# Seven products for eight over pairs of batches, and y moved by transfers

## The reference

```python
W = weights[condition]                        # 16 matrices of 64x64, one per batch
y = jnp.einsum('bct,bcd->bdt', x, W)          # 64 x 64 x 1024
gate_logits = jnp.einsum('bsd,ed->bse', y, gate_w)            # 8 experts
weights, selected = jax.lax.top_k(gate_logits, 2)
weights = jax.nn.softmax(weights, axis=2)
result = jnp.einsum('bsd,od->bso', y, base_w) + base_b        # 1024 x 1024
low = jnp.einsum('bsd,erd->ebsr', y, lora_A)                  # 8 experts of rank 16
lora_out = jnp.einsum('ebsr,eor,bse->bso', low, lora_B, w_full)
return x + result + 2.0 * lora_out
```

## Time and profile before

| | |
|---|---|
| median of 3 runs | 493.68 us (493.53 to 493.83) |
| the profiled execution's own time | 493.63 us |
| its span in the profile | 491.5 us |
| PE, ACT, DVE, POOL busy | 99%, 78%, 75%, 26% of the span |

### The profile page before, as it was taken

How to read it: one execution, slowest core, us unless ns; L and a number is a source line. 1 busy time by engine, 2 the same in 40 slices (tenths; PEclk the granted TensorE clock), 3 DMA queues, 4 the chain that set the end, 5 groups by cost and what they waited for, 6 DMA issues and landing times.

```text
span 491.5 us, 8738 instructions
## 1 busy us (share of the span) xinstructions
PE 487.2 (99%) x2771; PEld 478.5 (97%) x2771; DVE 371.0 (75%) x801; ACT 382.3 (78%) x740; POOL 129.4 (26%) x111
## 2 busy tenths in 40 slices
PE   9999999999999999999999999999999999999997
PEld 8999999999999999999999999999999999999996
DVE  4987878778787778787787777787877787777654
ACT  4888878878778887778787788887788877887620
POOL 2033302333113333033332223332133320233121
PEclk9999999999999999999999999999999999999999
DMA  8812122231221221221222222312213212211112
GB/s 334 353 43 74 74 91 96 55 97 59 87 91 64 85 96 52 92 91 53 96 64 82 89 79 70 96 53 91 91 53 96 84 62 88 96 54 55 55 44 85
DMA packets 31986, 43.89 MB, mean 89 GB/s; under 512 B 18402, under 2 KB 22370, under 8 KB 31970
## 3 DMA queue, kind: packets, MB, share of 16 engines
q1 hardware_dynamic: 31826, 43.17, 25.7%
q10 hardware_dynamic: 144, 0.52, 0.3%
HBM read 25.00 MB, written 18.68 MB: 89 GB/s over the span
## 4 chain that ended last, share of the span: by engine, by line
PE 93%; ACT 3%; DMA 2%; DVE 1%; SPq 0%; issue 0%; ACTq 0%
PE acc L658 79%; PE acc L691 9%; PE mixed L678 6%; DMA w_raw<-in_proj_w 2%; ACT y_moved L370 1%; ACT w_raw L362 1%; DVE w_raw L474 0%; ACT x_parts L357 0%; ACT w_hi_rows L343 0%; SPq L225 0%; SPq L221 0%; DVE y_turned L481 0%; ACT y_hi L393 0%; DVE w_raw L560 0%; SPq L218 0%
## 5 line engine op out<-in xcount | busy, mean ns | idle before, releaser
L658 PE MATMUL acc<-w_hi_rows,y_hi 128*128 128x384 f32 (+3 forms) x768 | 256.5, 337 | 0.1
L658 PE MATMUL acc<-w_hi_rows,y_lo 128*128 128x384 f32 (+3 forms) x768 | 256.4, 337 | 0.0
L658 PE MATMUL acc<-w_lo_rows,y_hi 128*128 128x384 f32 (+3 forms) x768 | 256.0, 337 | 0.0
L370 ACT COPY y_moved<-w_raw 32x256 f32<-32x256 f32 x480 | 194.2, 405 | 37.8 <-DVE w_raw L474 32.0
L302 POOL TENSOR_TENSOR w_raw<-x_sb,bias 128x1024 f32<-128x1024 f32 x32 | 77.0, 2409 | 344.2 <-DVE low L529 258.5
L658 PEld LDWEIGHTS acc<-w_hi_rows,y_hi 128*128 128x128 f32 x768 | 143.9, 188 | 3.7 <-ACT w_hi_rows L343 0.4
L658 PEld LDWEIGHTS acc<-w_lo_rows,y_hi 128*128 128x128 f32 x768 | 143.9, 188 | 3.1
L658 PEld LDWEIGHTS acc<-w_hi_rows,y_lo 128*128 128x128 f32 x768 | 143.9, 188 | 0.6 <-DVE y_lo L459 0.3
L474 DVE TENSOR_TENSOR w_raw<-mixed,w_raw 64x1024 f32<-64x1024 f32 x60 | 73.0, 1217 | 30.0 <-ACT w_raw L362 29.6
L481 DVE STREAM_TRANSPOSE y_turned<-y_moved 128x512 f32<-128x512 f32 x60 | 42.3, 706 | 51.5 <-ACT y_moved L370 51.5
L362 ACT COPY w_raw<-mixed 64x1024 f32<-64x1024 f32 x60 | 60.8, 1014 | 20.9 <-PE mixed L678 20.2
(11 more groups left out here) (56 smaller groups left out, 238.5 us busy)
## 6 DMA issues: line engine op xcount, KB each, us to landing
x_sb<-in_x SPq DMA_DIRECT2D x32, 512.0 KB, 3.5
out<-w_raw SPq DMA_DIRECT2D x31, 512.0 KB, 2.6
w_raw<-in_proj_w SPq DMA_DIRECT2D x8, 580.0 KB, 9.6
scratch<-low_squares SPq DMA_DIRECT2D x29, 64.0 KB, 1.5
lowT_raw<-scratch SPq DMA_DIRECT2D x116, 16.0 KB, 1.8
cw<-in_cond_w ACTq DMA_DIRECT2D x1, 512.0 KB, 3.6
lb_raw<-in_lora_b SPq DMA_DIRECT2D x1, 512.0 KB, 16.4
bias<-in_base_b SPq DMA_DIRECT2D x1, 512.0 KB, 17.1
```

Source lines behind the costliest of these rows:

```text
L370: done = nc.scalar.copy(y_moved[q * SQ:(q + 1) * SQ, g, :, :], piece.rearrange("m (k q a) -> m q k a", q=QUARTERS, a=SQ)[:, q, :, :])
L658: return nc.tensor.matmul(acc[:, c % 2, b, 0:hi - lo], y_part[:, c % 2, k, :], w_part[:, k, lo:hi], start=(k == 0 and product == 0), stop= ...
```

## The change

The kernel now goes in 16 *steps* of two pairs each (pair 0 and pair 1 of the step). On 256 + 136 = 392 columns (`plain`) both pairs are projected as before. On the other 768 columns, the two pairs (rows), two halves of k, and two blocks of 384 columns make a 2 x 2 by 2 x 2 product of blocks. Step 0 does it with eight products (`multiply`, 4 x 3 = 12 matmuls of 384 columns each), all later steps with seven, which need four sums of blocks of y (`make_sums`, on POOL), four sums of blocks of w (once, on POOL), four snapshots of a bank that is still summed up (`snap`, on ACT) and three additions of snapshots to `res` (`add_snaps`, `add_third`, `add_fourth`, on POOL).

```diff
+            def step(j, u, ahead=True):                      # PE
+                plain_pair(j, u, 0)
+                mix(j, u, 0)
+                plain_pair(j, u, 1).then_inc(plain_done, 1)
+                mix(j, u, 1)
+                pe.wait_ge(res_ready, 2 * s)
+                multiply(C22, half(0, 0), factor(B11)).then_inc(prod_done, 1)
+                multiply(C11, half(0, 1), factor(B21)).then_inc(prod_done, 1)
+                mix(j, u, 2)
+                multiply(C22, summed(S2), factor(T2), first=False).then_inc(prod_done, 1)
+                multiply(C21, half(1, 1), factor(T4)).then_inc(prod_done, 1)
+                mix(j, u, 3)
+                multiply(C22, summed(S3), factor(T3), first=False).then_inc(prod_done, 1)
+                multiply(C12, summed(S4), factor(B22)).then_inc(prod_done, 1)
+                multiply(C22, summed(S1), factor(T1)).then_inc(prod_done, 1)
...
+            def plain_pair(j, u, i):                         # PE
+                if i == 0:
+                    pe.wait_ge(tails_added, s)
...
+            def mix(j, u, i):                                # PE
+                pe.wait_ge(x_split, m + 1)
+                pe.wait_ge(sel_ready, 2 * m + 2)
+                if u > 0 or i > 0:
+                    pe.wait_ge(sum_done, m)
```

`mix` now takes 128 rows at once with a w_sel of high and low parts, two matmuls for each batch, four batches in a step. The sum of a pair goes to one buffer `y_sum`, and the 16 pieces are moved by 16 transfers on SP's queue:

```diff
-            def move(j, c, b, pieces):                       # ACT
-                act.wait_ge(sum_done, 8 * j + 2 * (c - 2) + b + 1)
-                for i in pieces:
-                    done = nc.scalar.copy(y_moved[q * SQ:(q + 1) * SQ, g, :, :],
...
+            def move(j, u, i):                               # SP
+                sp.wait_ge(sum_done, 4 * s + 2 * i + 2)
+                if u > 0 or i > 0:
+                    sp.wait_ge(turned, 4 * s + 2 * i)
+                for g in range(QUARTERS):
+                    for q in range(QUARTERS):
+                        sp.dma_start(y_moved[q * SQ:(q + 1) * SQ, g, :, :].rearrange("m k a -> m (k a)"),
+                                     y_sum[g * SQ:(g + 1) * SQ, q * RUN:(q + 1) * RUN]).then_inc(moved[i], 16)
...
+            def step(j, u, ahead=True, load=True):           # SP
+                store(j, u - 1, i)                           # i = 0, 1
+                sp.wait_ge(bias_added, 2 * s + i + 1)
+                load_x(j, 2 * u + 4 + i)                     # i = 0, 1
+                move(j, u, 0)
+                turn_low(j, u)
+                move(j, u, 1)
...
+            def rest(j, u, i):                               # ACT
+                act.wait_ge(mix_done, 4 * s + i + 1)
+                if i < 2 and u > 0:
+                    act.wait_ge(moved[1], 16 * MOVES * s)
+                if i >= 2:
+                    act.wait_ge(moved[0], 16 * MOVES * (s + 1))
+                nc.scalar.copy(y_sum[here, :]..., mixed[there, :, :]).then_inc(rest_ready, 1)
...
+            def make_sums(j, u):                             # POOL
+                pool.wait_ge(turned, 4 * s)
+                pool.wait_ge(prod_done, 7 * s)
...
+            def step(j, u, ahead=True, split=True):          # POOL
+                make_sums(j, u)
+                select(j, u, 2)
+                s_low(j, u, S3)
+                s_low(j, u, S1)
+                add_bias(j, u, 0)
+                add_bias(j, u, 1)
+                select(j, u, 3)
+                add_snaps(j, u)
+                select(j, u, 4)
+                select(j, u, 5)
+                add_third(j, u)
+                add_fourth(j, u)
```

More of the change, by code:

```diff
@@ L16 @@
 SCALING = 32.0 / 16.0
+BW = 384
+SQ = 32
+QUARTERS = P // SQ
+B11, B21, B22, T1, T2, T3, T4 = range(7)
+S1, S2, S3, S4 = range(4)
 def adaln_ffn_kernel(
@@ L272, in _ @@
-            for i in range(4):
-                sp.wait_ge(stored[i], 16 * (PAIRS // 4 + (2 if i == LAST % 4 else 0)))
+            step(0, LAST - 1, load=False)
+            step(0, LAST, ahead=False, load=False)
+            store(0, LAST, 0)
+            for n, cols in enumerate((slice(BW, O), slice(0, BW))):
+                sp.wait_ge(res_ready, 2 * LAST + 2 + n)
+                sp.dma_start(out_pairs[2 * LAST + 1, :, cols], res[:, 1, cols]).then_inc(stored[1], 16)
+            for i in range(2):
+                sp.wait_ge(stored[i], 16 * (STEPS + i))
@@ L328, in _ @@
+            step(0, 1)
             with pool.Fori(0, LOOPS) as j:
-                for u in (5, 6, 7, 8):
+                for u in (2, 3):
                     step(j, u)
-            for n in range(PAIRS - 3, PAIRS):
-                step(0, n, ahead=(n + 2 < PAIRS))
-            add_bias(0, LAST)
+            step(0, LAST - 1, split=False)
+            step(0, LAST, ahead=False, split=False)
         @block.scalar
@@ new lines, in _, with step @@
+            rest(0, 0, 1)
+            x_high(0, 0, 3)
+            t_high(2, T1)
+            lowT_high(0, 0)
+            rest(0, 0, 2)
+            t_high(3, T2)
+            y_high(0, 0, 0, 0)
+            y_high(0, 0, 0, 1)
+            rest(0, 0, 3)
+            t_high(4, T4)
+            x_high(0, 0, 4)
+            x_high(0, 0, 5)
+            y_high(0, 0, 1, 0)
+            y_high(0, 0, 1, 1)
+            def step(j, u, ahead=True, split=True):
+                s_high(j, u)
+                if ahead:
+                    rest(j, u, 0)
+                    x_high(j, u, 2)
+                    rest(j, u, 1)
+                gate_exp(j, u)
+                if ahead:
+                    x_high(j, u, 3)
+                snap(j, u, 0, 1)
@@ L441, in _ @@
+                if not ahead:
+                    snap(j, u, 2, 5)
+                lowT_high(j, u)
+                if ahead:
+                    rest(j, u, 3)
+                if split:
+                    x_high(j, u, 5)
+                if ahead:
+                    snap(j, u, 2, 5)
+                snap(j, u, 3, 7 if ahead else 6)
+                if ahead:
+                    y_high(j, u, 1, 0)
+                    y_high(j, u, 1, 1)
+            step(0, 1)
             with act.Fori(0, LOOPS) as j:
-                for u in (4, 5, 6, 7):
+                for u in (2, 3):
@@ new lines, in first_step, with all_experts @@
+                mix(0, 0, 2)
+                multiply(C22, half(1, 1), factor(B22)).then_inc(prod_done, 1)
+                mix(0, 0, 3)
+                multiply(C22, half(1, 0), (b12_hi, b12_lo), first=False).then_inc(prod_done, 1)
+                pe.wait_ge(lb_ready, 1)
+                pe.wait_ge(lowT_ready, 1)
+                all_experts()
+            def all_experts():
+                plain_experts()
+                for i in range(2):
+                    experts(i, C11 + 2 * i, 0, BW)
+                    experts(i, C11 + 2 * i + 1, BW, 2 * BW).then_inc(lora_done, 1)
```

1080 lines of the change are left out of this document (614 added, 466 removed).

## The result

The changed kernel takes 865.86 us (median of 3 runs, 863.71 to 868.42) against 493.68: a ratio of 1.7542, with an interval of 1.7465 to 1.7619. The sign was foretold, the size was not: 670 us was forecast, with 555 to 745 as its range. The profiled execution took 868.42 us, span 866.6.

The account below looks back on a forecast made before the run. PE bounded the kernel before; after the change a closed loop of waits, 41.0 us a period, would. 64 + 14 x 41.0 + 29.5 = 667.5, with 2.1 us outside the span 670 us; range 555 to 745.

Parts of the forecast that it names:

- The two waits of PE: PE's longest waits would be on `add_rest` ahead of a mix and on `tails_added` ahead of `plain_pair` 0.
- the landing: The last transfer of a move was to land 1.8 us after its issue.
- The rival in which PE stays the bound: The loop fits within PE's 27.75 us of work a step, total 463 us; chance 8%.
- item 5: Move 0 on SP: 16 transfers issued 0.40 us apart (bounds 0.32 and 0.46) plus 1.8 landing, 7.8 us.
- the same sum: Waits of one step added from turn to turn: period 41.0 us; the chain as summed, 595 to 725 us, chance 66%.
- Items 3, 4 and 8: Two `s_low` (2.4 us), two `add_bias` (4.8), then second load, move 0 at T = 13.3; port hindrance adds 2.6.
- the third rival: Ports and half clock on PE cost more: period 46.0 us from the ports, total 740 us; chance 13%.
- item 8: POOL and DVE hinder each other at SBUF ports: 2.6 us a period, bounds 0 and 7.6.
- Step 0 and the tail: First step, with weights, POOL's sums and `add_bias` to 39.2, ends at 64 us; last step, without moves, takes 29.5.

Follow-up runs that it names:

- the run before it: Changed kernel with the first move and the low-rank transfers put ahead of the two loads of x on SP's queue: 916.06 us, ratio 1.8551.
- the loop opened: Changed kernel with moves through DRAM, `y_sum` free once its store landed, calls reordered on all queues, `add_bias` behind the ranking: 604.31 us, ratio 1.2245.

## Why the prediction was right in kind and wrong in size

**Right.** PE was no longer the bound, and the loop from turn to turn through POOL, SP, DMA, ACT and DVE was. The two waits of PE, its share (65%), the small share of PE in the chain, the landing (1.84), the time between landing and next move (8.3 us; 7.4 forecast) and the sign came out. The rival in which PE stays the bound had nothing for it.

**The step that failed first is item 5, the price of an issue.** It was taken as 0.40 us with bounds of 0.32 and 0.46, from returns out of DRAM. From SBUF to SBUF it is 0.63 (0.59 for the transfer and 0.04 to the next), outside both bounds. That is 3.5 us a move, 7.0 a period, and 7 in step 0: 105 us, shown by the runs with half of the pieces and half of the bytes. With 0.63 in it the same sum gives 71 + 14 x 48.0 + 29.5 + 2.1 = 775 us, outside the range by this one term. My upper bounds for the issue and for the ports together give a period of 47.8, some 765 us; the range stopped short of them. My argument, that a short descriptor list doesn't cheapen an issue, held. What I didn't allow for was that the kind of transfer could make it dearer. The run through DRAM points to the pair, SBUF as source and SBUF as goal: the store of `y_sum` to DRAM (512 KB) issued in 0.34 us, and the four loads from DRAM into the same 32 partitions of `y_moved` in 0.43 each. Why this pair costs more stays open.

**Items 3, 4 and 8 named the wrong last wait ahead of move 0.** The sum let it wait for `bias_added`, at T = 13.3, with 2.6 for the ports. It waits for `add_rest` 1 behind the ranking on DVE, at T + 19.4. The 6.1 us between 13.3 and 19.4 lie in three places. The gather for mix 2 ends 2.5 later (T + 8.2), 1.5 of it because PE's 24 matmuls take 5.8 instead of 4.26 after the wait (the third rival had this term). POOL's two `s_low` and two `add_bias` take 8.7 instead of 7.2. And move 0 comes 2.5 us behind the end of `add_bias` instead of 0.4, because the ranking is held for 1.8 and 2.2 us. The held ranking stood in the upper bound of item 8 only, as 2.4 us; the run with `add_bias` behind it shows that it is paid in each step (3.9 us at the start of move 0, 4.1 in the period, against the run before it). But that run shows too that it isn't recovered alone: the load of x then comes late. So the third rival, ports and clock, was no rival to the sum but a part of it, and it was true beside the dear issue; I had the two as exclusive, so the range had no place for both.

**Step 0 and the tail.** `add_bias` ended at 52.95 in place of 39.2. POOL had begun its sums at 23.3, but between the third and the fourth it waited 5.7 us for a mix, and each of its operations was in POOL's order:

```profile
33.25 3.56 POOL L465 TENSOR_TENSOR t_raw<-t_raw 128x1536 f32<-128x1536 f32 x1
42.52 0.41 POOL L383 CAST w_sel<-cw_parts 128x64 fp32r x2 [5.71 <-PE mixed L950]
42.88 3.48 POOL L469 TENSOR_TENSOR t_raw<-snaps,t_raw 128x1536 f32<-128x1536 f32 x1
46.30 6.65 POOL L393 TENSOR_TENSOR res<-x_sb,bias 128x1024 f32<-128x1024 f32 x2
```

I had priced the sums (3.6 us, and 3.4 to 3.6 were measured for three of four) but followed POOL without the mixes that stand between them. Without them the first step is 14 us shorter (eight products). The tail was 7.7 us longer. In it I read the same held ranking, the return of the low-rank part through DRAM late by 2.7 us for PE, and half clock in the first matmuls; no run took them apart.

**What stays open.** The mean period is 52.94, of which the step read here explains 51.7. In the later steps the difference goes with the time of PE's first 24 matmuls, up to 1.4 us more than in this step; the longer first periods (57.8, 54.0) weren't followed. Why the period with `add_bias` late and with the move first is no shorter is read from the loads' waits, not tested with a load on another queue. Whether ACT's queue would issue SBUF transfers more cheaply than SP's wasn't tried.

**Where the expected gain went.** The 2.1 us of a step that seven products save on PE were never in reach: with the transfers as they are, PE isn't the bound, and seven cost 4.7 us a period more than eight; with the loop opened they still cost 27.6 us in all. Opening the loop gave back 262 us (865.9 to 604.3), eight products 28 more. The rest to the kernel before is 83 us. Of these 53 lie in the 14 periods (33.7 instead of 29.93): in the two steps shown above PE is idle for 2.9 us a step, mostly in waits for the sums and the splits of x, and busy for 1.2 us longer. The other 30 us lie in the first step and behind the last period, and no run took them apart.

## What to carry to other kernels

Before an engine's work is cut, draw the loop that the new waits close, and add it up with every issue of every transfer in it: here 32 issues at 0.63 us outweighed all that PE could save in a step by ten to one. The price of a transfer's issue must come from a transfer of the same kind; where the trace has none, the upper bound belongs well above the nearest row. Put operations of GpSimd that last microseconds where VectorE has nothing short on the path, and when an order is moved on one queue, look at once for the load that becomes late.

## What the hardware showed unexpectedly

- The issue of a transfer on SP's queue took 0.59 us (0.63 from one to the next) from SBUF to SBUF, and 0.43 for DRAM to SBUF in the same kernel; a store from SBUF to DRAM took 0.37; halving the bytes changed nothing in the kernel's time (865.9 and 864.3 us).
- A DVE operation on 128x16 elements lasted 2.33 us beside POOL's `add_bias`, and 0.17 us without it.
- Matmuls of 96 columns began 0.11 us apart at full clock and 0.21 at half, where 384 columns take 0.174 at full clock: a quarter of the columns took two thirds of the time. PE was busy with them without a break, and the granted clock was 0.50; with 384 columns in their place the mean clock of the run was 0.885.
